# A one-core attention and expert kernel: mask of the linear states on DVE instead of POOL, POOL's list in another order, sixteen token tiles prepared ahead instead of eight

## What is computed

```python
def reference(x, Wq, Wk, Wv, Wo, bo, router_w, w1, w2):
    xn = layernorm(x)
    return x + attn(xn) + ffn(xn)

# attn: 16 heads of 16. Heads 0 to 3: softmax in windows of 128 keys, with the window before.
# Heads 4 to 15: causal linear attention in blocks of 64 tokens:
    q = softmax(q, axis=-1); k = elu(k) + 1.0
    ctx = cumsum(einsum('bhund,bhune->bhude', bk, bv), axis=2)
    ctx = ctx / (bk_cumsum[..., None] + 1e-06)         # then shifted by one block
    attn = einsum('bhund,bhude->bhune', bq, ctx)

# ffn: each token goes to its two best experts
    scores = xf @ router_w.T
    top_v, top_i = top_k(scores, 2); routing_w = softmax(top_v)
    for e in range(8):
        w_e = sum(where(top_i == e, routing_w, 0.0))
        out += (gelu(xf @ w1[e].T) @ w2[e].T) * w_e[:, None]
```

## Time and profile before

| what | us |
|---|---|
| runs | 837.24, 829.16, 831.96 |
| median | 831.96 |
| the profiled execution, its own time | 835.22 |
| its span, first to last instruction | 833.4 |
| steps (first stage product to the first expert group) | 23.9 to 428.7 |
| mean granted TensorE clock over the span | 0.936 |

### The profile page before, as it was taken

The page is one execution under the profiler, slowest core; times in us unless marked ns, Lnnn a source line. Parts: engine busy times, 40 slices in busy tenths (PEclk is TensorE's granted clock), DMA queues, the critical chain, the costliest instruction groups (busy, mean ns, idle before and its releaser), DMA issues.

```text
span 833.4 us, 21487 instructions
## 1 busy us (share of the span) xinstructions
PE 713.3 (86%) x6866; PEld 560.7 (67%) x6867; DVE 422.1 (51%) x1540; ACT 407.0 (49%) x1115; POOL 426.0 (51%) x423
## 2 busy tenths in 40 slices
PE   1978787878679888887879999999999999999983
PEld 0645454545446555565558888888888888888763
DVE  6756565637776777756433333333333333334321
ACT  4756565656336666664533444444444444443331
POOL 6664646455335555557332555555555555544422
PEclk9988888989767999998869999999999999999998
DMA  7424231222211322222112444444444444443321
GB/s 246 127 80 125 71 109 60 94 71 71 63 53 39 83 81 80 82 85 84 42 48 47 77 76 76 76 76 76 76 76 76 76 76 76 77 70 59 58 45 20
DMA packets 87991, 64.26 MB, mean 77 GB/s; under 512 B 54675, under 2 KB 81556, under 8 KB 87924
## 3 DMA queue, kind: packets, MB, share of 16 engines
q1 hardware_dynamic: 73204, 43.69, 19.2%
q0 software_dynamic: 13632, 18.91, 14.2%
q10 hardware_dynamic: 1088, 0.79, 0.3%
HBM read 36.08 MB, written 17.96 MB: 65 GB/s over the span
## 4 chain that ended last, share of the span: by engine, by line
SPq 37%; issue 24%; POOL 17%; PE 9%; DVE 5%; DMA 5%; ACT 2%; POOLq 0%; DVEq 0%; ACTq 0%
SPq L688 36%; PE bank L279 4%; POOL stage L832 3%; POOL state L837 3%; POOL xb L825 2%; PE bank L1105 2%; POOL w2h L740 2%; DMA out<-attn,rows_to 2%; POOL atl L822 1%; POOL w2l L841 1%; DMA out<-res,rows_to 1%; POOL ke L815 1%; PE bank L1213 1%; POOL w1l L841 1%; DVE stats L1240 1%
## 5 line engine op out<-in xcount | busy, mean ns | idle before, releaser
L279 PE MATMUL bank<-stage,w1h 128*128 128x256 f16 (+1 forms) x1248 | 197.4, 265 | 4.9 <-DMA stage<-xin 3.6
L279 PE MATMUL bank<-stage,w1l 128*128 128x256 f16 (+1 forms) x624 | 163.7, 264 | 0.0
L1213 PE MATMUL bank<-w2h,pt 128*128 x568 | 154.9, 273 | 5.9 <-issue 4.8
L1213 PE MATMUL bank<-w2h,spare 128*128 x568 | 154.8, 273 | 0.0
L1213 PE MATMUL bank<-w2l,pt 128*128 x568 | 154.8, 273 | 0.0
L279 PEld LDWEIGHTS bank<-stage,w1h 128*128 x1248 | 114.4, 98 | 23.9 <-issue 7.5
L1024 ACT ACTIVATE pt<-ss 128x512 f16<-128x512 f32 (+1 forms) x78 | 41.8, 583 | 168.8 <-PE bank L1213 164.2
L874 POOL DMA_INDIRECT out<-res,rows_to x36 | 63.1, 1753 | 74.1 <-DMA stage<-rows 52.6
L874 POOL DMA_INDIRECT out<-attn,rows_to x35 | 61.0, 1744 | 73.0 <-DMA out<-attn,rows_to 46.2
L822 POOL TENSOR_TENSOR atl<-attn,ath 128x128 f16<-128x128 f32 x32 | 13.8, 430 | 165.3 <-ACT ath L957 165.3
L949 ACT ACTIVATE ss<-ss,negmax 128x256 f32<-128x256 f32 x128 | 63.5, 497 | 16.0 <-DVE negmax L1301 15.9
(11 more groups left out here) (242 smaller groups left out, 1679.0 us busy)
## 6 DMA issues: line engine op xcount, KB each, us to landing
stage<-w1c SPq DMA_DIRECT2D x16, 512.0 KB, 3.6
stage<-w2c SPq DMA_DIRECT2D x16, 512.0 KB, 3.5
w1h<-x SPq DMA_DIRECT2D x16, 256.0 KB, 3.8
xn_rows<-w2h SPq DMA_DIRECT2D x32, 128.0 KB, 3.2
xb<-x SPq DMA_DIRECT2D x32, 128.0 KB, 3.3
out<-res SPq DMA_DIRECT2D x32, 128.0 KB, 3.5
stage<-xin SPq DMA_TRANSPOSE x144
stage<-rows SPq DMA_TRANSPOSE x140
```

What stands on the lines that cost most here:

```text
L279: ins = pe.matmul(dst, lhs(a, k), rhs(c, k), start=(n == 0), stop=(n == len(terms) - 1))
L1213: ins = pe.matmul(bY[h][:, 0:D], (hh, hl)[a][:, f, h * P:(h + 1) * P], (w2h, w2l)[c][:, DS(which * (FC * D) + f * D, D)], start=(f == a == ...
```

## The change

The mask of the linear states moves from POOL to DVE, right behind the reciprocal. In POOL's list atl moves from ahead of xb to behind the stage product, directly ahead of the split. AHEAD goes from 4 to 8: eight pairs, sixteen tiles, are normalised, turned and routed before the steps start, and COPIED, TOTALS, RANKS, HOT and TABLE become steps 10, 11, 12, 13 and 25.

```diff
--- before.py
+++ after.py
@@ -60,7 +60,7 @@
 CB = 1 + GA
 VL = 2 * LD
 VC = VL + CTX
-AHEAD, WEIGHTS_AT = 4, 2
+AHEAD, WEIGHTS_AT = 8, 2
 SLOTS = 8
 PAIRS = TOK // 128 // 2
 DS = bass.ds
@@ -817,10 +817,6 @@
                         rstd_of(t.early(0)[0] // 2)
                     if t.has(-2):
                         b = t.row(-2)
-                        t.wait(s["loch_in"], -2)
-                        t.wait(s["pr_ps"], -4)
-                        pool.tensor_tensor(atl[b][:, 2 * P:3 * P], attn[b][:, 0:P], ath[b][:, 2 * P:3 * P],
-                                           ALU.subtract).then_inc(s["locl_in"], 1)
                         t.wait_dma(xb_loaded, -2)
                         pool.tensor_tensor(xb[b][:], xb[b][:], bias[:], ALU.add).then_inc(s["xb_in"], 1)
                     for u in t.early(1):
@@ -830,12 +826,12 @@
                         hi, lo = ((w1h, w1l), (w2h, w2l))[m]
                         t.wait(s["stage_hi"], 0)
                         pool.tensor_scalar(stage[m][:], stage[m][:], WS, 1.0, ALU.mult, ALU.mult).then_inc(s["stage_up"], 1)
-                    if t.has(-1):
-                        b = t.row(-1)
-                        t.wait(s["state1_in"], -1)
-                        t.wait(s["lin_ps"], -3)
-                        pool.tensor_tensor(state[b][:], raw[b][:], ctx_mask[:].unsqueeze(1).to_broadcast([P, 2, CTX]),
-                                           ALU.mult).then_inc(s["mask_in"], 1)
+                    if t.has(-2):
+                        b = t.row(-2)
+                        t.wait(s["loch_in"], -2)
+                        t.wait(s["pr_ps"], -4)
+                        pool.tensor_tensor(atl[b][:, 2 * P:3 * P], attn[b][:, 0:P], ath[b][:, 2 * P:3 * P],
+                                           ALU.subtract).then_inc(s["locl_in"], 1)
                     if t.has(0):
                         t.wait(s["stage_up"], 0)
                         pool.tensor_tensor(lo[:, DS(t.window(0) * F, F)], stage[m][:], hi[:, DS(t.window(0) * F, F)],
@@ -1360,6 +1356,9 @@
                         t.wait(s["state1_in"], -1)
                         dve.reciprocal(rden[b][:].rearrange("p g u -> p u g"), raw[b][:, :, 0:CTX:CTX - 1])\
                            .then_inc(s["rden_in"], 1)
+                        t.wait(s["lin_ps"], -3)
+                        dve.tensor_tensor(state[b][:], raw[b][:], ctx_mask[:].unsqueeze(1).to_broadcast([P, 2, CTX]),
+                                          ALU.mult).then_inc(s["mask_in"], 1)
                     for u in t.early(0):
                         scaled(u)
                     if HOT <= t.t < HOT + BATCHES:
```

## The result

| | before | after |
|---|---|---|
| median, us | 834.28 (829.16 to 837.24, 4 runs) | 862.41 (860.45 to 865.06, 4 runs) |
| the profiled execution, its own time | 835.22 | 860.45 |
| its span | 833.4 | 858.5 |
| mean granted clock | 0.936 | 0.913 |

The ratio is 1.0346, with a 95% interval of 1.0281 to 1.0411: slower. Forecast were 868 us (836 to 888) and slower by over 1% with a chance of 0.78.

The account below looks back on a forecast made before the run. Steps were taken as near TensorE's own time, so removed waits count until TensorE is full. Terms -17.5 + 35.6 + 29 + 1.5 - 2.4 - 8 - 2 gave +36 us on the 832.0 median: 868 us, range 836 to 888.

Parts of the forecast that it names:

- the one-hots: Steps 13 to 22, where DVE makes one-hot columns: 13.1 us each, 2.9 more than before, +29 us in all.
- the start: Prologue and steps up to the routing's start: routing begins at 180.6 instead of 198.09, 17.5 us earlier.
- the routing: Steps 10 to 12, bound by DVE's routing list: 0.5 us each for the mask, +1.5 us.
- the moved steps: Four attention steps left to do behind the earlier routing: 8.9 us each, +35.6 us (to 41).
- the table step: Step where POOL's four gathers hold up ke: ke about 2.5 us sooner, -8 us (-10 to -3).
- B: Steps 1 to 7: load lands before DVE asks, 10.4 us a step, 820 us in all; chance 0.03.
- A: Steps 13 to 22: one-hots finish before POOL's split, 9.6 us each, 833 us; chance with its variant (838) 0.17.
- D: Neither port nor clock costs: 15.6 us in early steps, 9.6 in late ones, 821 us; chance 0.05.
- C: TensorE's clock stays low: early steps 19.3 us, those with one-hots 14.7, 890 us; chance 0.13.
- Part 1: Mask on DVE: some 0.5 us there; steps without one-hots 8.9 us instead of 10.24, bounds 8.8 and 10.24.
- Part 2: POOL's new order: atl and split stop DVE's one-hots; 13.1 us a step in steps 13 to 22, +29 us.
- Part 3: Eight pairs ahead: prologue +12.7 us, late x loads make early steps 18.1 us, routing 17.5 us earlier, four steps behind it.

Follow-up runs that it names:

- The last run: Mask on DVE, POOL's old order, six one-hot columns first, three pairs ahead, gathers moved behind ke of the next step, against the kernel before: 772.1 us, ratio 0.929.

## Why the prediction was right, and where it was not

*Right in kind and nearly in size.* Forecast +36 us, measured +25.1 between the two profiled spans and +28 between the medians. Both causes were named and each is shown by a run that takes it away alone: the load, -46 us, and the split, -21 to -24. The number is closer than its terms. Against the two spans the forecast is 11 us too high, from terms that were 18 us too high together (most of it the one-hots, the start, the routing and the moved steps) and others 7 too low (above all the table step); that so much cancelled is luck. So rivals B (the load is no wait) and A (the split is not met) are out, D too, with granted clocks of 0.81 and 0.86 in these steps, and C, since neither an early step nor one with one-hots reached its 19.3 and 14.7 us on average.

*Part 1.* The mask was to take 0.5 us on DVE; it takes 0.53 where nothing meets it, and 0.84 in steps 2 to 7, which prepare a pair. Steps without one-hots were to take 8.9; they take 8.38. The lower bound, "8.8 (TensorE full)", was misread: the late step of the earlier trace rows, 286.70 to 296.94, is one with one-hots, and 0.37 of its 8.80 busy microseconds are the six matmuls (L396) that turn the columns. A step without one-hots has no such matmuls, and 8.43 is close to the 8.40 measured. The same step served as the period before, which for steps without one-hots was 10.18 (step 28).

*Part 2.* Forecast 13.1 us a step, measured 12.8 on average from the second to the tenth, with the wait of 2.7 us for 2.9 forecast. The term of +29 was nonetheless too large: the ten steps together became 20.8 us longer (106.2 to 127.0). I had set 10.24 against all ten, while the first of them took 13.9 us before (245.9 to 259.8), and 12.0 after. That is the first mis-sized term, 8.2 us too high: 4.8 of them come from this step, which got 1.9 us shorter instead of 2.9 longer, and 3.4 from the other nine, which became 2.5 us longer each. As forecast, two one-hot instructions were left when the split began, and atl's meeting was small. The full-stop reading of DVE's L528 in the earlier trace rows is borne out by the steps shown above: a one-hot instruction of 0.25 us took 2.17 beside the split of 2.11. The Trainium skill, "SBUF — State Buffer", section "Who interferes with whom", has one exclusive lock for the whole instruction; these rows agree.

*Part 3, start and early steps.* The chain from the result to the statistics was forecast at 6.9 us and took 6.4 (102.76 to 109.13), the step 18.1 and took 18.06 on average. The result of step 8 came at 157.0 (159.8 forecast), the routing at 176.7 (180.6). The 17.5 us of earlier start were 21.4: 2.6 of the difference come from the start, 1.1 from steps 8 and 9, which load nothing and took 9.6 and 10.1 instead of 10.4. How the start splits into terms depends on the order in which the runs are set side by side. With the mask on POOL, eight pairs move the result of step 3 by 22.6 us (47.7 to 70.3), where 24.2 were forecast, and mask and new order then give 3.6 back (66.7), where 2.6 were forecast. With the mask on DVE, four more pairs cost only 7.9 us (53.8 to 61.7 with early loads) and the late loads of steps 1 and 2 another 5.0, but the 53.8 is itself 6.1 later than before: there TensorE ran from 40 to 50 us at 0.50, before at 0.86. So these two numbers hold a difference of the clock too.

*Steps behind the routing.* Four moved steps cost 33.5 instead of 35.6; the first three with routing were 0.6 shorter, not 1.5 longer; the two behind the one-hots brought 3.3, not 2.4.

*The table step, the step of the working that failed.* I forecast -8 us because "with mask and xb out of the way ke comes about 2.5 us sooner and most of the low stretch goes". The step behind the gathers took 15.5 us instead of 16.0, and the one before it, in which they start, 8.9 instead of 11.0: -2.6 in all. POOL in the changed kernel, then TensorE:

```profile
379.97 0.95 POOL L360 DMA_INDIRECT rows<-xn_rows,tables  x1 [0.30 <-issue]
380.94 0.60 POOL L815 TENSOR_TENSOR ke<-ke,krelu 128x192 f32<-128x192 f32 x1
```

```profile
381.59 0.80 PE L1068 MATMUL bank<-val,ke 64*128 64x129 f32 x2 [2.70 <-issue]
```

The first half of the reason held: TensorE's product with ke starts 13.5 us after the result of step 25, before the change 16.1 (388.73 in the earlier trace rows, less 372.59), so 2.6 us sooner. What failed is the second half. TensorE comes to this product 2.1 us sooner too; 1.60 of that is its wait for the mask in this step, which is gone. TensorE before the change:

```profile
380.93 0.44 PE L1084 MATMUL bank<-state,qgt 128*64 128x128 f32 x4 [1.60 <-POOL state L837]
```

So it still stands 2.70 us instead of 3.20, and then still runs at 0.51 (383 to 392 us; 0.56 in the earlier trace rows). Ke stands directly behind the gathers, as before. The last run fits: with ke in front of the gathers the step fell from 13.75 to 8.88 us.

The steps behind the table and the end gave 2.9 us, 2 forecast, and 1.7 were lost after the last result. The sum of what was measured, in the order start, steps 10 to 12, one-hots, the two behind them, the step with the gathers, the one behind, moved steps, end, rest: -21.4 - 0.6 + 20.8 - 3.3 - 2.1 - 0.5 + 33.5 - 2.9 + 1.7 = +25.2, against 25.1 between the spans.

## What to carry to other kernels

A longer look-ahead is worth only the distance between a transfer's issue and its use. Here it shortened this distance, because the slots were used up: read in the issuing engine's list in which step a load is issued once the distance equals the number of buffers. A rearranged list on one engine must be laid beside the list of the engine whose instructions it can stop, and a removed wait is worth what stands in no other wait's shadow. A run for each part of a change, and one for each repair, shows this where their sum doesn't.

## What was not expected of the hardware

- DVE and POOL took turns: in the kernel with the mask alone three one-hot instructions were stopped one after another by three POOL instructions, one each, and every one ended 0.04 to 0.05 us after its POOL instruction. These are tensor_scalars of 128 and 72 fp16 columns with one source tile. The mask, a tensor_tensor with both sources in SBUF, grew from 0.53 to 1.14 us beside POOL's stage product. Qgt, with PSUM as a source, went through beside the split in its usual 0.41 us.
- A wait of TensorE cost more than its length. 2.62 us in a step of 13.76 cost 4.1. With the late load TensorE idles 5.67 us of 17.60 instead of 0.53 of 9.90, so 5.1 more, and the step is 7.7 us longer. The rest is busy time, 11.93 instead of 9.37, at granted clocks of 0.88 and 0.81 in these steps and 1.00 without the wait.
- A later start of an instruction can pay: holding POOL's split back by 1.1 us gave 2.6 us a step.
